# Window attention: the causal mask moved from VectorE's reduction into TensorE's accumulation, and a new order of the window stages

## The reference

```python
def local_attention(q, k, v):            # windows of 128 tokens, 8 heads of 64
    bq = q.reshape(b, h, w, WINDOW, d) * QK_SCALE
    bk, bv = look_around(bk), look_around(bv)     # the window before and this one: 256 keys
    sim = jnp.einsum('bhwid,bhwjd->bhwij', bq, bk)
    mask = (i < j) | (i > j + WINDOW) | (j == -1)
    sim = jnp.where(mask, -jnp.finfo(sim.dtype).max, sim)
    attn = jax.nn.softmax(sim, axis=-1)
    return jnp.einsum('bhwij,bhwjd->bhwid', attn, bv)

def _layer(x, ...):
    q, k, v = ...                        # shift_token(x) @ wqkv, in heads
    q, k = rotary_xpos(l2norm(q) * qs, l2norm(k) * ksc)
    x = x + local_attention(q, k, v) @ wo
    ...                                  # layer norm, gated MLP
for l in range(2):
    x = _layer(x, ...)
```

## Time and profile before

| | |
|---|---|
| Time, median of 3 runs | 2272.52 us (2271.97 to 2272.78) |
| The profiled execution's own time | 2272.78 us |
| Its span, first to last instruction | 2270.3 us |
| PE busy | 2129.8 us (94%), 13992 matmuls |
| DVE busy | 1674.2 us (74%) |
| ACT busy | 1503.3 us (66%) |
| POOL busy | 1334.1 us (59%) |
| Granted TensorE clock, mean | 0.957 |

### The profile page before, as it was taken

How to read it: one execution, slowest core, us unless ns; L and a number is a source line. 1 busy time by engine, 2 the same in 40 slices (tenths; PEclk the granted TensorE clock), 3 DMA queues, 4 the chain that set the end, 5 groups by cost and what they waited for, 6 DMA issues and landing times.

```text
span 2270.3 us, 44803 instructions
## 1 busy us (share of the span) xinstructions
PE 2129.8 (94%) x13992; PEld 1483.5 (65%) x13992; DVE 1674.2 (74%) x3989; ACT 1503.3 (66%) x3418; POOL 1334.1 (59%) x1376
## 2 busy tenths in 40 slices
PE   3899999999999999979999999799989999997998
PEld 2444444444444444337888887688778888886887
DVE  4777788777878888548888887466378888874675
ACT  2277778777888888646777777454367777774443
POOL 0444556433335443477888876455368888874775
PEclk7699999999999999789999999899999999998999
DMA  7667776755666666325445454100054545541111
GB/s 163 97 123 146 142 142 133 151 146 127 149 142 155 152 162 142 122 76 141 108 105 116 102 110 98 59 17 6 10 137 103 117 104 107 114 99 35 50 58 42
DMA packets 192617, 244.71 MB, mean 108 GB/s; under 512 B 26072, under 2 KB 110792, under 8 KB 192392
## 3 DMA queue, kind: packets, MB, share of 16 engines
q1 hardware_dynamic: 189832, 233.47, 46.4%
q0 software_dynamic: 2560, 8.39, 1.0%
HBM read 93.28 MB, written 59.24 MB: 67 GB/s over the span
## 4 chain that ended last, share of the span: by engine, by line
PE 79%; DMA 6%; POOL 4%; SPq 3%; issue 3%; ACT 3%; DVE 2%; POOLq 0%; ACTq 0%; DVEq 0%
PE PS L479 14%; PE PS L481 13%; PE PS L480 13%; PE PS L600 9%; PE PS L584 8%; PE PS L693 5%; PE PS L669 5%; PE PS L567 4%; PE PS L678 4%; DMA KS<-hs 3%; PE PS L653 3%; SPq L1496 2%; DMA hs<-HL 2%; POOL TM L1254 1%; ACT PT L821 1%
## 5 line engine op out<-in xcount | busy, mean ns | idle before, releaser
L997 DVE TENSOR_REDUCE MX<-PS 128x1 f32<-128x512 f32 x1024 | 642.7, 682 | 168.4 <-PE PS L567 158.1
L821 ACT ACTIVATE PT<-PS 128x512 f32<-128x512 f32 x1024 | 546.1, 599 | 142.9 <-PE PS L584 140.9
L567 PE MATMUL PS<-KS,QS 48*128 48x512 f32 x1024 | 356.2, 453 | 46.5 <-DMA KS<-hs 36.1
L584 PE MATMUL PS<-QS,KS 50*128 50x512 f32 x1024 | 389.4, 462 | 5.9 <-ACT PT L821 5.5
L584 PEld LDWEIGHTS PS<-QS,KS 50*128 50x128 f32 x1024 | 166.4, 189 | 274.5 <-issue 215.5
L1369 POOL TENSOR_TENSOR PB<-PB,RC 128x512 f32<-128x512 f32 (+1 forms) x256 | 260.1, 1037 | 95.8 <-DVE RC L1117 95.8
L600 PE MATMUL PS<-PT,VP 128*17 128x512 f32 x2048 | 278.0, 615 | 2.9 <-ACT OT L828 2.8
L884 ACT ACTIVATE PB<-PB,NMf 128x256 f32<-128x256 f32 (+1 forms) x512 | 243.0, 479 | 14.3 <-DVE NMf L1108 13.8
L567 PEld LDWEIGHTS PS<-KS,QS 48*128 48x128 f32 x1024 | 170.8, 191 | 110.9 <-issue 59.8
L1108 DVE CUSTOM_DVE_ANT_0 PB<-PS,mk 128x256 f32<-128x256 f32 (+1 forms) x512 | 176.2, 382 | 60.2 <-PE PS L669 60.0
L1349 POOL TENSOR_TENSOR RI<-RI,mhalf 128x8 f32<-128x8 f32 x128 | 213.4, 1667 | 10.7
(11 more groups left out here) (183 smaller groups left out, 5110.3 us busy)
## 6 DMA issues: line engine op xcount, KB each, us to landing
qT<-QN SPq DMA_DIRECT2D x384, 128.0 KB, 2.3
hs<-HL SPq DMA_DIRECT2D x64, 512.0 KB, 3.9
kT<-kT SPq DMA_DIRECT2D x256, 128.0 KB, 2.5
QS<-hs SPq DMA_DIRECT2D x192, 128.0 KB, 6.0
KS<-hs SPq DMA_DIRECT2D x192, 128.0 KB, 8.5
od<-OT SPq DMA_DIRECT2D x64, 256.0 KB, 5.8
OC<-od SPq DMA_DIRECT2D x32, 256.0 KB
cst<-rs SPq DMA_DIRECT2D x32, 256.0 KB
```

What stands on the lines that cost most here:

```text
L567: pe.matmul(PS[:, bank, :], QS[rows, s, h // 2, qt * P:(qt + 1) * P], KS[rows, s, h // 2, :], start=True, stop=True).then_inc(fills("amax" ...
L584: pe.matmul(PS[:, bank, :], KS[rows, s, pair, kt * P:(kt + 1) * P], QS[rows, s, pair, :], start=True, stop=True).then_inc(fills("score", v ...
L821: act.activation(PT[:, kt % 2, 2 * i + half], PS[:, TURNS["score", vb, g, kt, half, i][0], :], ACT.Exp).then_inc(drains("score", vb, g, kt ...
L997: dve.tensor_reduce(MX[:, vb % 2, h // 8, qt, c:c + 1], PS[:, TURNS["amax", vb, h, qt][0], :], AX, ALU.max).then_inc(drains("amax", vb, h, ...
```

## The change

The change has two parts.

First, the mask. A new DVE stage `window_consts`, once in the last step of the head, copies the mask twice (one copy for each head of a pair) and the identity into bf16. `wscore` then begins with one more matmul for each pair of heads, the identity times the mask, over both heads at once: 512 columns, or 256 in the first window of a sequence. The four score matmuls add onto it. They now go by part of q first and then by head. `wmax` is no longer two custom operations but one reduction over both heads straight from PSUM, 128x512 to 128x2, that writes nothing to `PB`. `wexp` reads the scores from PSUM and writes `PB`, and it, not `wmax`, releases the bank. With that, `wexp` takes over the wait for the transposes of unit u - 2 that read the same `PB`, and `wrecip` waits for the bank's release in place of the semaphore `expd`.

Second, the order. `WINDOW_ORDER` is another table, with the same 63 kinds and parts, other places and in part other lags: `wval`, `wsum` 1 and `wrot` 1 go from lag -2 to -1, `wpt` 0 and 1 from 0 to 1, `woh` and `wout` from 1 to 2, both chores change too.

```diff
@@ LAST_STEP
-    (10, "rot", (0,)), (11, "add_bo", (NV - 2,)),
+    (10, "window_consts", ()), (10, "rot", (0,)), (11, "add_bo", (NV - 2,)),
@@ WINDOW_ORDER (63 entries each, all rewritten; the first line of each)
-    ("wres", None, 2), ("wexp", 2, 1), ("wqk", 0, -2), ("wv", None, -1), ("wscore", 0, 0), ("wrn", 0, -2), ("wqkt", 0, -1),
...
+    ("wsum", 1, -1), ("wval", None, -1), ("wpt", 0, 1), ("wrot", 1, -1), ("woh", None, 2), ("wpt", 1, 1), ("wout", None, 2), ("wres", None, 2),
...
@@ tensors
-        sb("room4", [P, 320], F32)
+        mask = sb("mask", [P, 2, 256], BF16)
+        identbf = sb("identbf", [P, P], BF16)
@@ wscore (PE)
+                if L == 0 and u == 0 and hp == 0:
+                    pe.wait_ge(sem["mask"], 3)
...
+                pe.matmul(out[:, :, k0:], identbf[:], mask[:, :, k0:], start=True, stop=False, skip_group_check=True)
-                for h in range(2):
-                    for x in range(2):
-                        m = pe.matmul(out[:, h, k0:], qT[:, u % 2, x, h, hp], kT[:, hp, h, keys], start=x == 0, stop=x == 1)
+                for x in range(2):
+                    for h in range(2):
+                        m = pe.matmul(out[:, h, k0:], qT[:, u % 2, x, h, hp], kT[:, hp, h, keys], start=False, stop=x == 1, skip_group_check=True)
@@ wexp (ACT)
-                act.wait_ge(*drained("wscore", L, u, hp))
+                act.wait_ge(sem["negmax"], nth("wmax", L, u, hp))
                 if u >= 2:
+                    act.wait_ge(*filled("wpt", L, u - 2, hp))
                     act.wait_ge(sem["recip"], nth("wrecip", L, u - 2, hp // 2))
-                for hh in (2 * hp, 2 * hp + 1):
-                    p = PB[:, u % 2, hh, k0:]
-                    m = act.activation(p, p, ACT.Exp, bias=NMf[:, u % 2, hh:hh + 1], scale=-1.0, accum_out=SUM[:, u % 2, hh:hh + 1])
-                m.then_inc(sem["expd"], 1)
+                for h in range(2):
+                    hh = 2 * hp + h
+                    m = act.activation(PB[:, u % 2, hh, k0:], out[:, h, k0:], ACT.Exp, bias=NMf[:, u % 2, hh:hh + 1],
+                                       accum_out=SUM[:, u % 2, hh:hh + 1])
+                m.then_inc(drains("wscore", L, u, hp), 1)
@@ window_consts (DVE, new)
+                dve.wait_ge(sem["mask_in"], 16)
+                for i in range(2):
+                    dve.tensor_copy(mask[:, i], mk[:]).then_inc(sem["mask"], 1)
+                dve.tensor_copy(identbf[:], ident[:]).then_inc(sem["mask"], 1)
@@ wmax (DVE)
-                for h in range(2):
-                    hh = 2 * hp + h
-                    m = dve.tensor_tensor_reduce(out=PB[:, u % 2, hh, k0:], in0=out[:, h, k0:], in1=mk[:, k0:], scale=-1.0, scalar=3e38, op0=ALU.add,
-                                                 op1=ALU.min, accum_out=NMf[:, u % 2, hh:hh + 1])
-                m.then_inc(drains("wscore", L, u, hp), 1)
+                dve.tensor_reduce(NMf[:, u % 2, 2 * hp:2 * hp + 2], PS[:, bank, :].rearrange("p (h k) -> p h k", h=2)[:, :, k0:], AX, ALU.max,
+                                  negate=True).then_inc(sem["negmax"], 1)
```

More of the change, by code:

```diff
@@ L153 @@
 WINDOW_ORDER = (
-    ("wres", None, 2), ("wexp", 2, 1), ("wqk", 0, -2), ("wv", None, -1), ("wscore", 0, 0), ("wrn", 0, -2), ("wqkt", 0, -1),
[L155 to L162, removed]
+    ("wsum", 1, -1), ("wval", None, -1), ("wpt", 0, 1), ("wrot", 1, -1), ("woh", None, 2), ("wpt", 1, 1), ("wout", None, 2), ("wres", None, 2),
+    ("wqk", 0, -2), ("wadd", 1, -1), ("wexp", 2, 1), ("wrn", 0, -2), ("wrecip", 1, 1), ("wv", None, -1), ("wmax", 0, 0), ("wexp", 3, 1),
+    ("wscale", 0, 0), ("wscale", 1, 0), ("wptc", 0, 1), ("wptc", 1, 1), ("wsum", 0, -2), ("wqn", 0, -2), ("chore", None, -1),
+    ("wsq", 0, -2), ("wqkh", 0, -1), ("wswap", (0, 0), -1), ("wscore", 0, 0), ("wqkl", 0, -1), ("wswap", (0, 1), -1), ("wrn", 1, -2), ("wexp", 0, 0), ("wqkt", 0, -1), ("wqkh", 1, -1), ("wswap", (1, 0), -1),
+    ("wptc", 2, 1), ("wmax", 1, 0), ("wqkl", 1, -1), ("wswap", (1, 1), -1), ("wscore", 1, 0), ("wrot", 0, -2), ("wrecip", 0, 0), ("wqkt", 1, -1),
+    ("wexp", 1, 0), ("wptc", 3, 1), ("wadd", 0, -2), ("wpv", 0, 1), ("wpt", 2, 1), ("wmax", 2, 0), ("wpt", 3, 1), ("wqn", 1, -2),
+    ("wscale", 2, 0), ("wscale", 3, 0), ("wsq", 1, -2), ("chore_lo", None, 1), ("wscore", 2, 0), ("wtr", None, -2), ("wtrl", None, -2), ("wtrh", None, -2), ("wmax", 3, 0), ("wol", None, 1), ("wqk", 1, -2), ("wscore", 3, 0), ("wpv", 1, 1),
 )
@@ L1101, in wmax @@
                 if u >= 2:
-                    dve.wait_ge(*filled("wpt", L, u - 2, hp))
-                if L == 0 and u == 0 and hp == 0:
-                    dve.wait_ge(sem["mask_in"], 16)
-                out = PS[:, bank, :].rearrange("p (h k) -> p h k", h=2)
-                for h in range(2):
-                    hh = 2 * hp + h
-                    m = dve.tensor_tensor_reduce(out=PB[:, u % 2, hh, k0:], in0=out[:, h, k0:], in1=mk[:, k0:], scale=-1.0, scalar=3e38, op0=ALU.add,
-                                                 op1=ALU.min, accum_out=NMf[:, u % 2, hh:hh + 1])
-                m.then_inc(drains("wscore", L, u, hp), 1)
+                    dve.wait_ge(*drained("wscore", L, u - 2, hp))
+                dve.tensor_reduce(NMf[:, u % 2, 2 * hp:2 * hp + 2], PS[:, bank, :].rearrange("p (h k) -> p h k", h=2)[:, :, k0:], AX, ALU.max,
+                                  negate=True).then_inc(sem["negmax"], 1)
             def wrecip(L, u, g):
-                dve.wait_ge(sem["expd"], nth("wexp", L, u, 2 * g + 1))
+                dve.wait_ge(*drained("wscore", L, u, 2 * g))
+                dve.wait_ge(*drained("wscore", L, u, 2 * g + 1))
                 if u >= 2:
@@ L1223, in fnorm @@
                 m.then_inc(sem["fnormed"], 1)
-            does = dict(begin=begin, split_w=split_w, tr_lo=tr_lo, mix=mix, mix_sum=mix_sum, heads_lo=heads_lo, amax=amax, fold=fold, inv=inv, res=res, stats=stats, norm_last=norm_last, rot=rotations, split_qkv=split_qkv, wzero=wzero,
+            does = dict(begin=begin, split_w=split_w, tr_lo=tr_lo, mix=mix, mix_sum=mix_sum, heads_lo=heads_lo, amax=amax, fold=fold, inv=inv, res=res, stats=stats, norm_last=norm_last, window_consts=window_consts, rot=rotations, split_qkv=split_qkv, wzero=wzero,
                         wtrl=wtrl, wrot=wrot, wsum=wsum, wadd=wadd, wqkl=wqkl, wmax=wmax, wrecip=wrecip, wol=wol, wres=wres, mzero=mzero, mstat=mstat,
```

7 lines of the change are left out of this document (5 added, 2 removed).

## The result

| | before | after |
|---|---|---|
| Time, median | 2271.97 us (2266.16 to 2287.65, 7 runs) | 2301.26 us (2294.43 to 2307.01, 7 runs) |
| Ratio | | 1.0122, 95% interval 1.0091 to 1.0155 |
| Profiled execution, its span | 2272.78, 2270.3 us | 2298.41, 2296.2 us |

The change makes the kernel slower, as forecast, but by 1.2% (28 us; 21 to 35 by the interval) and not by 2.2% (50 us). The measured 2301 us lies 5 us under the range of 2306 to 2358.

A forecast was written before the change was run, and what follows sets the result against it. The prediction took TensorE's streamed columns to bound the window stages. To the profiled 2272.78 us it added 52.2 for the mask matmuls and took off 1.9 for units beside waits: 2323 us, about 2.2% slower, range 2306 to 2358.

The forecast's parts named there:

- What bounds the kernel: Window stages: the columns TensorE streams bound a unit of 12.3 us, not a chain through the other engines.
- I take the nearest rows: Mask matmul priced at float32r start-to-start distances: 192 x 0.233 + 64 x 0.117 = 52.2 us.
- One unit of each of the two layers comes off: First and last units of each layer, where TensorE waits anyway: 2 x 0.93 us of mask matmul deducted.
- I take zero, with 10 us either way: New order of the window stages: only waits in the dense stretch, either way at the ends; counted as nothing.
- the rearrangement I named: Stage ends: last unit's `wout` behind the MLP's first transposes may shorten the 5.4 us wait by a few us.
- DVE and ACT: Window units: DVE gains under 0.1 us four times a unit, ACT's exponentials from PSUM cost the same; both counted nothing.
- The type change: bf16 identity between float32r weights: taken as zero, upper end 33 us; as a rival 2356 us, chance 7%.
- The bank hold: Scores' PSUM bank held some 1.8 us, not 0.75; cover ample; rival of POOL or held bank making TensorE wait: 13%.
- The signs I named: Dense stretches: L667 0.23 us before scores, unit 12.3 to 13.1 us, TensorE busy about 50 us more, above 99%.
- POOL as the bound: Rival inside the unit: TensorE waits perhaps 0.6 us for POOL's scaling, 38 us, 2361 us; 13% with held bank.
- The cheap matmul: Rival for the mask matmul: bf16 at half the price per column, 26 us, total 2297 us; chance 6%.
- Not slower: Rival at the window stages' starts and ends: new order closes waits, up to 54 us, to 2269 us; chance 4%.

## Why the prediction was wrong

**What bounds the kernel: right.** Dense units are bound by the columns that TensorE streams. Taking the mask matmul out or doubling it moves twenty units by 15.5 and 14.8 us, and taking work off DVE and ACT moves them by 0.6 at most.

**"I take the nearest rows": 52.2 us for 256 mask matmuls; nearly right.** Measured in the blocks it is 0.209 us between transposes and about 0.238 beside float32r for 512 columns, 0.11 and 0.13 for 256. In dense units that is 0.76 us a unit, 64 x 0.76 = 48.6 us, where 52.2 would be 0.82. This term was 3.6 us too large. By the Trainium skill's figure in "TensorE: Matmul & The Clock Gate", "Back-to-back issue gap" (216 ns for N=512), the sum was 48 us, which the traces bear out; its sustained 131 ns for N=512 they do not: the second of two copies in a row costs 0.217.

**"One unit of each of the two layers comes off": the step that failed.** I took 1.9 us off for work beside waits. The run without the mask matmul shows 48.6 - 39.1 = 9.5 us hidden, and the doubled one hides as much again of its second copy. Not one unit of each layer comes off but six, the first two and the last four: 12 x 0.76 = 9.1 us. 54 us of missing busy time at the ends is more than two units can hold, and should have told me. A part of the hidden work stands where TensorE waited anyway, as I had argued; for the rest TensorE had less time at half clock, which I had left out of the account wholly. These are single profiles whose starts scatter by up to 4 us, so the 9.5 is good to a few us; that the doubled kernel shows it again makes it more than scatter.

**"I take zero, with 10 us either way" for the order: too low as a best guess, inside its bound but for one profile with 11 us.** The new order is worth 4 to 11 us behind the head, 4 to 5 at equal clock. In the dense units it saves 0.5 us of 246. At the ends the rearrangement I named is there. Timeline of PE after the change, where the first window stage ends (L712 the MLP's transposes, then `wout` at half clock):

```profile
1440.07 2.11 PE L680 MATMUL PS<-ident,PB 128*128 128x128 f32 x8 [6.19 <-POOL PB L1376]
1442.11 1.97 PE L695 MATMUL PS<-PTB,V 128*64 128x128 f32 x16
1444.02 1.69 PE L712 MATMUL PS<-ident,HN 128*128 128x128 f32 x8
1450.78 0.58 PE L478 MATMUL PS<-WOF,OTr 128*128 128x256 f32 x1 [5.08 <-DVE OTr L1128]
...
1453.51 0.63 PE L478 MATMUL PS<-HT,W 128*128 128x512 f32 x1
```

The MLP's transposes now run before the last output projection, and the MLP's matmuls begin right behind it. The wait ahead of the MLP, 5.4 us in the earlier trace rows, is gone; 5.1 us stand before `wout` instead. What lies between the last scores and the MLP shrinks from 28.4 us to 25.1 and 24.4, but one of the three profiles of before has 25.5. That one has 8.9 us at half clock there, the two with 28.4 and 28.3 have 16.4 and 16.5, the changed kernel's 11.6 and 10.8, the order alone 11.3 and 12.3 with 25.2 and 26.1 us. So most of the shrinking goes with the clock, and that the moved wait itself saves time was not shown.

**The sum behind the head**: 50.3 forecast, less 3.6 for the rate, 7.6 for what the ends hide beyond my 1.9, 4.2 for the order and the rest of the code, gives 34.9, as measured. Set on the median of before that is 2307 us, inside my range. The timed median is 6 us lower still, and that part goes with the clock: the changed kernel's executions had a median clock of 0.9655 against 0.960, 23 us less at half clock, which at 0.33 us each is 7 us (an estimate). In the profiles the head, which the change leaves alone, has 102 and 108 us at half clock after the change and 109, 116 and 131 before, so at least a part of this is luck; where the timed executions had it is not on record. My 0.2% for what can be told from no change was too small as well: the kernel before alone runs from 2257.75 to 2288.09 us. Most of the fault lies with the sum even so, since without the 15 us above the forecast would have stood 6 us from the result and not 22.

**What I costed at nothing.** DVE and ACT: right within 0.6 us in twenty units; DVE went from 276.5 to 249.8 us busy in 320 and nothing followed. The type change: nearly right, zero beside transposes and 0.03 us beside float32r. The bank hold: hidden in the new order, as the walk through the table had it, and up to 0.67 us a unit in the old one, so the cover I named was real.

**The signs I named.** The mean unit came out at 13.02 us and TensorE's share above 99%, as forecast. Its busy time rose by 35 to 47 us (2126.4, 2129.8 and 2131.8 before, 2165.0 and 2173.1 after) and not by 50; the first of the two profiles after the change lacks the records of 76 of the 256 mask matmuls. L667 was to stand 0.23 us ahead of the first score matmul and stands 0.03 ahead; only the length of the whole block shows the 0.21.

**The rivals.** POOL as the bound did not happen: no wait of PE for POOL in the dense stretch. The cheap matmul did not either. "Not slower" was wrong in its extent only: its mechanism, waits at the ends that take up the new work or close, accounts for 14 us at most where 50 were needed.

## What to carry to other kernels

When one engine is dense, an added instruction costs its start-to-start distance, read from the nearest like instruction; but multiply it only by the units in which that engine has no wait, here 52 of 64, and look unit by unit where these begin and end. Moving a mask from an engine with room to the engine that bounds is a loss whatever it simplifies, and a reordering that comes in the same change can hide a part of that loss: run each alone. When an untouched part of the program differs between two profiles, take more profiles before explaining a total, compare part by part, and compare the timed runs at an equal granted clock.

## What the runs showed of the hardware

DVE's sum of the rotated halves (SBUF to SBUF, 128x512) has two durations. In the kernel before it takes 1.08 us at 1208.67 and 0.68 at 1213.88. Of 128 such sums, the 59 of 0.9 us and more are all covered by POOL's scaling of P for at least 0.96 us, the short ones lie beside POOL's power or nothing. By form, 1060 to 1380 us, the mean was 0.871; after the change:

```profile
L1100 DVE TENSOR_TENSOR RA<-RA,RB 128x512 f32<-128x512 f32 x49 | 33.1, 675 | 0.0
```

With the new table and the old code it is 0.675 too, with the old table and the new code 0.898. The new order does not move the two engines' operations apart: 53 of the sums still have a scaling beside them for 0.4 us and more, and take 0.66 to 0.69 us. What differs is which starts first. In the kernel before the typical long sum starts 0.50 us after a scaling, ends 0.55 us after that scaling's end, and takes 1.09 us. In the changed kernel the sum starts 0.13 to 0.16 us ahead of the scaling, and now the scaling is the long one: 1.40 us in the median, where a scaling of 128x512 with no sum beside it takes 1.04. So in these traces the operation that starts later is the longer one. That was not tested by itself, and on this path it cost nothing.

Four float32r score matmuls of 128 columns take almost as long as four of 256: from the last transpose to the next group it is 0.506 against 0.586 us, about 0.10 and 0.12 each. Half the columns do not give half the time there.

The exponential of 128x256 takes 0.479 us from PSUM and 0.507 from SBUF:

```profile
L889 ACT ACTIVATE PB<-PS,NMf 128x256 f32<-128x256 f32 x149 | 69.8, 479 | 0.0
```
